# Edge counts of a graph: sorted edges and one-hot products in place of scatters to DRAM tables

## What is computed

```
adj  = zeros(N, N).at[src, dst].set(1)                # layer 0: attention along the edges only
a    = (x Wq + bq) (x Wk + bk)^T / sqrt(D)
attn = softmax(a * adj + (1 - adj) * NEG)
x    = x + attn @ (x Wv + bv);   x = x + experts_top2(layernorm(x))

neigh = segment_sum(x_n[src], dst)                    # layer 1: sums along the edges, repeated ones counted
x     = x + gnn_mlp((1 + eps) * x_n + neigh);   then attention of 8 heads, experts_top1, two layernorms
```

## Time and profile before

| | |
|---|---|
| median of 3 runs | 1212.32 us (1208.69 to 1212.51) |
| the profiled execution, its own time | 1207.77 us |
| its span, first to last instruction | 1205.4 us |
| mean granted TensorE clock | 0.850 of full speed |
| busy: TensorE / VectorE / ScalarE / GpSimd | 857.3 / 645.3 / 410.3 / 583.5 us |
| scatters on GpSimd (line 547) | 136, 217.2 us busy |
| share of the chain that ended last: TensorE / VectorE / GpSimd / transfers | 43 / 22 / 16 / 9% |

### The profile page before, as it was taken

One profiled execution on the slowest core, in us unless ns is written; L12 is line 12 of the kernel. 1 busy time (PEld: TensorE's weight loads), 2 busy tenths in 40 slices (PEclk: granted clock), 3 DMA queues, 4 the chain that ended last, 5 costly groups with the idle time before them and its releaser, 6 DMA issues.

```text
span 1205.4 us, 13123 instructions
## 1 busy us (share of the span) xinstructions
PE 857.3 (71%) x4216; PEld 674.6 (56%) x4216; DVE 645.3 (54%) x1291; ACT 410.3 (34%) x664; POOL 583.5 (48%) x386
## 2 busy tenths in 40 slices
PE   3176779900198679942978988899999987736980
PEld 2165558800176348931867766677777766522870
DVE  4544433000266954437252257678787786796547
ACT  0111112100244515522221204666565665532450
POOL 1378788888312025510162214668677765531340
PEclk9977779955599659975989988999999999965895
DMA  9722331222785414452321104001010050153334
GB/s 274 136 22 19 21 36 1 0 0 0 170 232 190 176 53 141 152 188 75 127 61 44 35 35 110 22 19 53 18 27 1 19 157 0 71 201 102 115 117 148
DMA packets 78730, 101.48 MB, mean 84 GB/s; under 512 B 29120, under 2 KB 51904, under 8 KB 77136
## 3 DMA queue, kind: packets, MB, share of 16 engines
q1 hardware_dynamic: 51856, 76.52, 20.5%
q0 software_dynamic: 26816, 24.20, 11.3%
HBM read 65.50 MB, written 31.00 MB: 80 GB/s over the span
## 4 chain that ended last, share of the span: by engine, by line
PE 43%; DVE 22%; POOL 16%; DMA 9%; issue 7%; ACT 3%; SPq 0%; DVEq 0%; POOLq 0%; ACTq 0%
PE PS L296 27%; POOL edge_table L547 15%; DMA edge_table<-count,index 5%; PE PS L1770 3%; PE PS L1785 3%; DVE neg_max L1381 3%; PE PS L1759 2%; DVE APL L937 2%; PE PS L1784 2%; PE PS L1609 2%; DMA edge_table<-zeros 2%; PE PS L1637 1%; DVE XN L970 1%; DVE W2L L937 1%; DMA CT<-edge_table 1%
## 5 line engine op out<-in xcount | busy, mean ns | idle before, releaser
L547 POOL DMA_INDIRECT edge_table<-count,index x136 | 217.2, 1597 | 85.3 <-issue 37.3
L631 POOL TENSOR_SCALAR AP__176<-AP__176,rden 128x1024 f32<-128x1024 f32 x64 | 182.0, 2847 | 86.5 <-DVE rden L1386 85.9
L559 POOL CAST WH<-RAW 128x512 fp32r<-128x512 f32 x30 | 23.0, 767 | 165.3 <-PE PS L296 95.5
L1381 DVE TENSOR_REDUCE neg_max<-PS 128x1 f32<-128x1024 f32 x64 | 78.2, 1222 | 37.1 <-PE PS L1759 36.1
L663 ACT ACTIVATE APH<-PS 128x512 fp32r<-128x512 f32 x128 | 71.7, 597 | 70.2 <-PE PS L1770 45.6
L937 DVE TENSOR_TENSOR APL<-PS,APH 128x512 fp32r<-128x512 f32 x128 | 82.8, 678 | 23.7 <-ACT APH L663 23.6
L296 PE MATMUL PS<-XTH,WH 128*128 128x512 f32 x224 | 88.0, 442 | 6.4 <-DVE XTL L937 6.4
L583 POOL DMA_INDIRECT BX<-normalised,gather_i x38 | 38.0, 1000 | 108.9 <-DVE scatter_i L1223 84.2
L296 PE MATMUL PS<-XTL,WH 128*128 128x512 f32 x224 | 84.2, 425 | 0.0
L296 PE MATMUL PS<-XTH,WL 128*128 128x512 f32 x224 | 81.8, 413 | 0.0
L1770 PE MATMUL PS<-ident,AP__176 128*128 128x128 f32 x512 | 71.1, 281 | 11.6 <-DVE APL L937 10.8
(11 more groups left out here) (261 smaller groups left out, 2328.1 us busy)
## 6 DMA issues: line engine op xcount, KB each, us to landing
edge_table<-zeros SPq DMA_DIRECT2D x2, 4096.0 KB, 22.9
YT<-expert_rows SPq DMA_DIRECT2D x12, 512.0 KB, 6.6
CT<-edge_table SPq DMA_DIRECT2D x8, 512.0 KB, 6.0
CT<-edge_table POOLq DMA_DIRECT2D x8, 512.0 KB, 7.1
counts<-CT SPq DMA_DIRECT2D x8, 512.0 KB, 6.8
W1R<-in_L_ffn_w SPq DMA_DIRECT2D x8, 512.0 KB, 7.8
W2R<-in_L_ffn_w SPq DMA_DIRECT2D x8, 512.0 KB, 5.6
normalised<-XN SPq DMA_DIRECT2D x2, 2048.0 KB, 8.6
```

The lines of the kernel that those rows point to most:

```text
L547: gp.indirect_dma_start(out=tables[r], out_offset=bass.IndirectOffsetOnAxis(ap=index[:, c:c + 1], axis=0), in_=count[:, c:c + 1], in_offse ...
L631: gp.tensor_scalar(AP_[:, i % 4, :], AP_[:, i % 4, :], rden[:, i % 4:i % 4 + 1], None, ALU.mult).then_inc(B["norm"], 1)
L1381: v.tensor_reduce(out=neg_max[:, i % 4:i % 4 + 1], in_=banks(2 * (i % 2)), axis=X_AXIS, op=ALU.max, negate=True).then_inc(B["mx"], 1)
```

## The change

The two tables, their zeroing, the scatters and the transfers of counts into `CT` are gone. On chip instead:

- **Sort.** VectorE finds for each edge the tile of 128 sources it belongs to (src >> 7) and, with a scan and two small matmuls for the offsets of partitions, its place in an order in which each tile's edges fill whole blocks of 128. There are 144 blocks (`EDGE_BLOCKS`).
- **Move.** For each of the 136 edge columns VectorE makes a one-hot of the place's lane (128 wide) and two one-hot rows of its block (144 wide) scaled by the source row + 1 and by dst; one matmul (288 columns, fp16) accumulates them in PSUM bank 7. Four columns are a quad: three quads before each of the last six Q/K blocks, two before each of the eight V tiles.
- **Count.** 144 one-hots of the source row (128 wide) are made beside the scores. Then in two passes, one for each half of the 1024 columns, VectorE makes 144 one-hots of dst (512 wide), four to a group in two buffers, and TensorE multiplies both and accumulates into the PSUM bank of the block's tile, which it takes from a register; it loads 24 registers before every sixth group. Even tiles are copied to `CT` by ScalarE, odd ones by VectorE.
- **Moved.** `CT` holds all eight tiles. SP loads x first, in two halves; it stores all counts behind the counting; the expert biases and `b2` are loaded after those. GpSimd's tables for the routing are made in the first stage. ScalarE waits for the stores before it writes `W1H`. The loops of the Q/K stage are written out.

The diff, cut to its core:

```diff
@@ sync
-        wait(setup, 1)
-        for r in range(TABLES):
-            sp.dma_start(tables[r][0:N * N, :]..., zeros...).then_inc(tables_clear[r], 16)
-            sp.dma_start(tables[r][N * N:N * N + P, :], zeros[:, 0:1]).then_inc(tables_clear[r], 16)
-        sp.dma_start(X[:, :, :], a["x"].rearrange("(t p) d -> p t d", p=P)).then_inc(x_in, 16)
+        for h in range(2):
+            sp.dma_start(X[:, 4 * h:4 * h + 4, :],
+                         a["x"][h * HALF:(h + 1) * HALF, :].rearrange("(t p) d -> p t d", p=P)).then_inc(x_in[h], 16)
...
+        wait(columns_used, 2 * COUNT_GROUPS)
+        for t in range(NT):
+            wait((counted_act, counted_dve)[t % 2], NT // 2 + t // 2 + 1)
+            sp.dma_start(counts_d[t * P:(t + 1) * P, :], CT[:, t, :]).then_inc(A["stored"], 16)
         expert_biases("L0_ffn_b1")
-        for t in range(NT):
-            if t >= 4:
-                count_out(t - 4)
-            count_in(t)
+        for m, n in enumerate(("L0_ffn_b2", "L1_ffn_b2")):
+            sp.dma_start(b2[:, m, :], a[n]).then_inc(cols_in, 16)
@@ gpsimd
+        gp.iota(columns16[:, :], pattern=[[1, N]], base=0, channel_multiplier=0, ...).then_inc(setup, 1)
...
-                gp.indirect_dma_start(
-                    out=tables[r], out_offset=bass.IndirectOffsetOnAxis(ap=index[:, c:c + 1], axis=0),
-                    in_=count[:, c:c + 1], in_offset=None, compute_op=ALU.add).then_inc(scattered[r], 16)
-            gp.dma_start(CT[:, t % 4, :], tables[1]..., accum_op=ALU.add).then_inc(A["summed"][t % 4], 16)
@@ scalar
+        for r in range(2):
+            act.wait_ge(columns_used, COUNT_GROUPS * (r + 1))
+            for t in range(0, NT, 2):
+                copy(CT[:, t, r * HALF:(r + 1) * HALF], PS[:, t, :], counted_act)
@@ vector
+        def quad(q):
+            if q >= 2:
+                v.wait_ge(edges_moved, q - 1)
+            for j in range(4):
+                c = slice(4 * q + j, 4 * q + j + 1)
+                v.tensor_scalar(edge_lanes[:, q % 2, j, :], lanes1[:, :], edge_lane[:, c], None, ALU.is_equal)
+                v.tensor_scalar(edge_values[:, q % 2, j, 0, :], blocks16[:, :], edge_block[:, c], src_f[:, c], ALU.is_equal, ALU.mult)
+                got = v.tensor_scalar(edge_values[:, q % 2, j, 1, :], blocks16[:, :], edge_block[:, c], dst_f[:, c], ALU.is_equal, ALU.mult)
+            got.then_inc(edges_picked, 1)
+        for i in range(2 * KT):
+            for _ in range(QUADS_IN[i]):          # (0, 0, 3, 3, 3, 3, 3, 3) + (2,) * 8
+                quad(done)
+                done += 1
+            v.wait_ge(Q0["hi"], i + 1)
+            lo_biased(dst[:, n, :], banks(2 * (i % 2)), bias[:, n:n + 1], hi_[:, n, :], Q0["lo"][i % 2])
+            v.wait_ge(w_hi, i + 5)
+            lo(WL[:, i, :], RAW[:, j, :], WH[:, i, :], w_ready)
         for t in range(NT):
+            for _ in range(QUADS_IN[2 * KT + t]):
+                quad(done)
+                done += 1
             v.wait_ge(Q0["v_hi"], t + 1)
             lo(VL[:, t, :], PS[:, t % 4, :], VH[:, t, :], Q0["v_done"])
...
+        for r in range(2):
+            for g in range(COUNT_GROUPS):
+                k = COUNT_GROUPS * r + g
+                if k >= 2:
+                    v.wait_ge(columns_used, k - 1)
+                for j in range(4):
+                    b = 4 * g + j
+                    got = v.tensor_scalar(count_columns[:, k % 2, j, :], columns16[:, r * HALF:(r + 1) * HALF],
+                                          block_column[:, b:b + 1], None, ALU.is_equal)
+                got.then_inc(columns_ready, 1)
+            v.wait_ge(columns_used, COUNT_GROUPS * (r + 1))
+            for t in range(1, NT, 2):
+                v.tensor_copy(CT[:, t, r * HALF:(r + 1) * HALF], PS[:, t, :]).then_inc(counted_dve, 1)
@@ tensor
+        for r in range(2):
+            for t in range(NT):
+                if r:
+                    pe.wait_ge((counted_act, counted_dve)[t % 2], t // 2 + 1)
+                elif t == 4:
+                    pe.wait_ge(Q0["s_done"], NT)
+                pe.matmul(PS[:, t, :], count_rows[:, EDGE_BLOCKS - 1, :], columns16[:, 0:HALF], start=True, stop=True)
+            for g in range(COUNT_GROUPS):
+                if g % 6 == 0:
+                    pe.load(tiles, block_tile[0:1, 4 * g:4 * g + 24])
+                    held = [pe.snap(q, min_val=0, max_val=NT - 1) for q in tiles]
+                pe.wait_ge(columns_ready, COUNT_GROUPS * r + g + 1)
+                for j in range(4):
+                    b = 4 * g + j
+                    got = pe.matmul(PS[:, ds(held[b % 24]), :]..., count_rows[:, b, :],
+                                    count_columns[:, (COUNT_GROUPS * r + g) % 2, j, :], start=False, stop=False, ...)
+                got.then_inc(columns_used, 1)
```

## The result

The changed kernel takes **1297.47 us** (median of 4 runs, 1294.31 to 1300.2), the kernel before beside it 1212.07 (4 runs): ratio **1.071, 95% interval 1.0674 to 1.0746**. It is slower by 85 us. The profiled execution took 1294.31 us with a span of 1292.6, against 1207.8 and 1205.4 before. The first mask (VectorE, line 1082 now) starts at 409.38 instead of 320.74, 88.6 us later. From there to the end of the span it is 883.2 us against 884.7. So the whole difference lies ahead of that mask, as the prediction laid it out.

A forecast was written before the change was run, and what follows sets the result against it. Scatters held up the first mask by 78 us, and zeroing delayed the start. Start -34, Q/K +24, V +76, scores +4, scatter wait -78, counting +118, about +109, less 2: 1315, plus 4.5 against the median 1319; range 1265 to 1365.

The forecast's parts named there:

- case A: Whole kernel: the forecast itself, 1319 us, 1285 to 1340 with the scatter of its terms; chance 0.52.
- Rival B: VectorE's quads and counting one-hots: 2-byte inputs also run only two elements a cycle, 1352 us; chance 0.15.
- nothing overlaps: Q/K loop: quads, columns and low parts run in turn, 19.6 us for each of six periods with quads.
- Rival E: Q/K and V stages: quads hidden under the matmuls of the stage before, 118 us gone, 1201 us; chance 0.05.
- the columns, taken at 7.75 us: Q/K period: the stretch of projection columns takes 7.75 us (81.52 to 89.27), as before.
- The last quad's tail: Q/K period: 1.1 us for the last quad's four 288-column matmuls (0.24 each) and a semaphore.
- the twelve matmuls start at 1.2 GHz: V tile: after gaps of some 7 us the matmuls start at the low clock and take 4.9 of 12.6 us.
- Table zeroing: Start: 8 MB of zeros ahead of x are gone; projections start at 30 instead of 64, 34 us earlier.
- the prediction's price for two inputs: VectorE operations: two inputs of 512 elements 0.61 us, fitting 1.04 ns an element plus 0.075 us fixed.
- the load with 3.2 us until the next matmul: Counting: 3.2 us from a register load's start to the next matmul, bounds 1.2 and 4, in a 9.1 us cycle.
- Rival C: Counting: TensorE at 1.2 GHz as each load idles the array some 2.3 us, cycle 11.4, 1347 us; chance 0.13.
- Rival D: Quads and counting: 0.16 us per quad operation (-19), loads of 1.2 us and no handshake (-25), 1275 us; chance 0.12.

The follow-up runs named there:

- experiments 1 and 2: Changed kernel, TensorE's quads moved behind the same tile's projection: first in Q/K loop alone (1240.57 us) or V loop alone (1244.54 us), then in both (1192.05 us).
- experiment 2: Changed kernel with TensorE's quads behind the same tile's projection in both Q/K and V loops: 1192.05 us, ratio to before 0.9855.

## Why the prediction was right, point by point

Forecast 1319, measured 1297.5: 21.5 too high, inside the range and inside the scatter given for case A (1285 to 1340). The stage ends, predicted and measured:

| | predicted | measured |
|---|---|---|
| Q/K starts | 30 | 27.9 |
| Q/K ends | 164 | 155.4 |
| V ends | 264 | 250.7 |
| scores end | 312 | 296.1 |
| counting | 118 | 113.3 |
| first mask | 430 | 409.4 |

- **The price of VectorE's operations** was right to 0.01 us. The prediction took 0.166, 0.228 and 0.266 us. It had read the only one-input row, which was fp32, as 8 bytes a cycle and carried that over to 2-byte operands. Measured from start to start, the kernel after:

```profile
98.59 0.25 DVE L1024 TENSOR_SCALAR edge_lanes<-lanes,edge_lane 128x128 f16<-128x128 f16 x1
98.75 0.31 DVE L1025 TENSOR_SCALAR edge_values<-blocks,edge_block,src_f 128x144 f16<-128x144 f16 x1
98.98 0.31 DVE L1026 TENSOR_SCALAR edge_values<-blocks,edge_block,dst_f 128x144 f16<-128x144 f16 x1
99.21 0.25 DVE L1024 TENSOR_SCALAR edge_lanes<-lanes,edge_lane 128x128 f16<-128x128 f16 x1
...
101.06 0.25 DVE L1024 TENSOR_SCALAR edge_lanes<-lanes,edge_lane 128x128 f16<-128x128 f16 x1
```

  0.16, 0.23, 0.23; four times that is 2.47 (98.59 to 101.06) against 2.49. The 512-element one took 0.263 without waits. Rival B (two elements a cycle) falls. The Trainium skill, "VectorE: DVE Perf Modes", section "The perf-mode tier table (the rule you actually need)", gives `tensor_scalar` on SBUF 4x for bf16; by these rows fp16 runs at that rate too.
- **The order of the lists** was the step that carried the forecast ("nothing overlaps"), and experiments 1 and 2 show it: with the same work in another order both stages are bound by VectorE. Rival E named 118 us; 103.7 were to be had by order alone. What it needed was not quicker quads but that TensorE's wait for them stand behind its matmuls. The prediction held against this rival that VectorE works in order and has quads(t) behind lo(t-1); experiment 2 left exactly that as it was, and the loss went. Of the two orders that "nothing overlaps" rested on, TensorE's was the dear one. The prediction gave the rival 0.05, which was right for this code.
- **Q/K**: the periods alternate between 18.3 (78.51 to 96.79) and 19.25, mean 18.8, not 19.6. The term that was mis-sized most is the columns, taken at 7.75 us: they took 6.6 in the one kind of period (88.62 to 95.3) and 7.6 in the other (106.90 to 114.5), by how soon their matmuls came from 0.43 to 0.23 apart. The last quad's tail with its semaphore is 0.9 us, not 1.1. Six periods make 5 of the 6.5 us by which the stage was predicted too long; the rest is in the tiles without quads.
- **V**: 95.3 us against 100. The step "the twelve matmuls start at 1.2 GHz" was half right. In one tile eleven of twelve ran 0.43 apart; in the next five or six did and the rest 0.23 apart, so tiles alternate between 12.4 and 11.4 us.
- **Start**: 36.1 us earlier, 34 predicted. The size was right, its reasons in part not. "Table zeroing" is 20 us of data and 12 of single-word writes. And the forecast let VectorE wait for x, landing near 12; in the trace it never waits for x. It starts at 4.03, when GpSimd's tables are ready (5.5 was allowed), sorts until 8.51 and goes on to the statistics without a stop, since x's two halves landed some 5.6 and 8.2 us after their issues near 2. The sorting operations took 4.5 us, not 3.4, with the scan of 1088 elements at 2.42 us, about twice what the prediction's price for two inputs gives. So the scan lay on the path, and it was some luck that the earlier tables and the earlier x made up for it: the statistics end at 15.0, for 15.4 forecast.
- **Scores**: 45.4 us for 48; VectorE's 144 one-hots (23.5 us) lay beside them as said.
- **Counting**: 113.3 against 118, cycle 8.74 against 9.1. The least certain term in it was the load with 3.2 us until the next matmul; it was 2.6 at the stage's start (296.2 to 298.80). That VectorE is idle during a load for want of buffers was the prediction's own step, and it was right: eight buffers took 32 us away. What it missed is that the load itself need not cost the array anything. Rival C, a cold clock while counting, falls: the granted clock was 0.95.
- **Rival D** (1275, loads of 1.2 us and no handshake, operations at the fixed cost) lies nearly as close to the result as A by its total (22.5 us off against 21.5), so the total alone can't choose between the two. The terms do: only the smaller load gap went D's way, and not by much.

The error of 21.5 is thus a sum of small ones of one sign: 2 at the start, 6.5, 4.7 and 2.6 in the next three stages, 4.7 in counting, and 1 behind the first mask and between profile and median. Nothing large cancelled between the stages; within the start two errors did.

## What to carry to other kernels

When work is moved onto an engine pair that already hands tiles back and forth, write down for each tile which engine's list waits for which, before adding up durations: here the same one-hots made the kernel 104 us longer when TensorE's wait for them stood ahead of its own matmuls than when it stood behind them. Two engines that need 6.9 us each for a unit and share two buffers took 8.7; with eight they took 6.3, and a 1.6 us register load between them no longer set the time. Where no engine of a stage is over 60% busy, as in both stages here, look for turns being taken before looking for a dear operation.

## What the runs showed of the hardware

- A register load of TensorE (24 values) takes 1.62 us in its queue. Behind a wait that the array must meet first it costs 1.5 to 1.9 us of idle array; with matmuls queued ahead, nothing (120 matmuls 0.232 apart on average across four or five loads).
- 2-byte one-hots of 512 elements cost VectorE 0.263 us each. With a semaphore wait that is only just met in each group of four they cost 0.286, about 0.09 us more for the group; that the wait is the reason is inferred from the two kernels' lists.
- A scan over 1088 fp32 elements took 2.42 us, while a two-input operation over as many took 1.29. The Trainium skill, "DVE: opcode table, instruction layouts, handler registers and perf-mode slots", section "6. Datapath and trigger behaviour", says of the built-in scan that it runs at half throughput; this row agrees.
- GpSimd and VectorE hinder each other on these one-hots in a lopsided way. GpSimd took 1.56 us for 512 elements with VectorE idle. From 198 to 203 us GpSimd kept that pace and VectorE fell to 0.5 us an operation (10 in 5 us); from 226 to 231 VectorE ran at 0.24, while one GpSimd operation took 15.1 us. The Trainium skill, "SBUF — State Buffer", section "SBUF: two separate sides", calls the port pair that the two share an exclusive lock, held for a whole instruction. That one of them is shut out fits; that GpSimd stays shut out through more than 50 instructions of VectorE in a row, as in the 15.1 us from 225.8, a lock held for one instruction does not explain by itself.
- 128 single-word writes to DRAM, of 0.5 KB in all, left the queue next to idle for some 4.5 us (5 to 16 GB/s from 16.5 to 21), and two such transfers put the end of the first stage 12 us later.
